# First loop of a four-layer graph network in fp32: the order of scores, attention times vectors, residual updates, low parts and stores

## The reference

```python
h = relu(layernorm(x))                                       # before each layer
x += softmax_over_nodes(rowsum((h Wq) * (adj (h Wk))) / sqrt(512)) * (h Wv)     # layer 0
w = adj * exp((h Wq + bq)(h Wk + bk)^T);  x += (w / rowsum(w)) (h Wv + bv)      # layer 1
x += Wo . attention with 8 heads, scores times 2 adj                            # layer 2
x += relu(H0 W0 + (T H) W1 + (T T H) W2 + biases), T from adj and a leaky relu  # layer 3
```

## Time and profile before

| | |
|---|---|
| median of 3 runs | 2211.23 us (2210.95 to 2213.39) |
| profiled execution | 2211.67 us, of it 2209.9 us from first to last instruction |
| TensorE busy | 2195.3 us, 99% |
| VectorE, ScalarE, GpSimd busy | 1306.4, 780.1, 721.7 us |
| granted TensorE clock | 1.00 |

### The profile page before, as it was taken

One profiled execution on the slowest core, in us unless ns is written; L12 is line 12 of the kernel. 1 busy time (PEld: TensorE's weight loads), 2 busy tenths in 40 slices (PEclk: granted clock), 3 DMA queues, 4 the chain that ended last, 5 costly groups with the idle time before them and its releaser, 6 DMA issues.

```text
span 2209.9 us, 39185 instructions
## 1 busy us (share of the span) xinstructions
PE 2195.3 (99%) x15756; PEld 1762.6 (80%) x15756; DVE 1306.4 (59%) x2712; ACT 780.1 (35%) x1393; POOL 721.7 (33%) x926
## 2 busy tenths in 40 slices
PE   8999999999999999999999999999999999999999
PEld 5788888888888888888888888888887777777776
DVE  4576666665665576655555555555676555555542
ACT  3433333233323333333332333332444444444432
POOL 1443433343443422432332323332353131213120
PEclk9999999999999999999999999999999999999999
DMA  6333323333333344433333323323452323232411
GB/s 211 78 80 98 101 84 98 90 93 92 86 93 94 106 136 127 113 86 93 86 101 95 112 82 91 92 82 101 139 162 81 120 73 121 74 120 72 123 46 58
DMA packets 142007, 220.53 MB, mean 100 GB/s; under 512 B 33920, under 2 KB 40064, under 8 KB 141824
## 3 DMA queue, kind: packets, MB, share of 16 engines
q1 hardware_dynamic: 135680, 209.62, 32.6%
q10 hardware_dynamic: 6144, 8.40, 1.6%
HBM read 84.71 MB, written 50.37 MB: 61 GB/s over the span
## 4 chain that ended last, share of the span: by engine, by line
PE 97%; SPq 1%; DMA 1%; DVE 1%; issue 0%; POOL 0%; ACT 0%; DVEq 0%; ACTq 0%
PE bank L327 54%; PE bank L317 32%; PE bank L343 3%; PE bank L563 2%; PE bank L499 1%; PE bank L469 1%; PE bank L364 1%; SPq L1001 1%; PE bank L307 1%; PE bank L549 0%; DVE hs L649 0%; DMA mcolt<-in_nodemask_cols 0%; DMA wq<-in_L_gnn_Wq_w 0%; DMA si<-rowsT 0%; DMA sirows<-si 0%
## 5 line engine op out<-in xcount | busy, mean ns | idle before, releaser
L327 PE MATMUL bank<-w_hi,h3T_hi 128*128 128x512 f32 x768 | 302.4, 394 | 0.0
L327 PE MATMUL bank<-w_hi,h3T_lo 128*128 128x512 f32 x768 | 299.0, 389 | 0.0
L327 PE MATMUL bank<-w_lo,h3T_hi 128*128 128x512 f32 x768 | 298.8, 389 | 0.0
L1008 ACT ACTIVATE Z<-bank 64x512 f32<-64x512 f32 x256 | 151.9, 593 | 273.3 <-PE bank L327 168.7
L624 DVE BATCH_NORM_STATS2 stA<-x 128x6 f32<-128x512 f32 x192 | 128.1, 667 | 114.8 <-DMA x<-in_x 106.5
L1022 ACT ACTIVATE hn<-x,stA 128x512 f32<-128x512 f32 x192 | 141.6, 823 | 119.1 <-POOL stA L1269 119.1
L649 DVE STREAM_TRANSPOSE hs<-hn 128x512 f32<-128x512 f32 x192 | 124.5, 690 | 87.6 <-ACT hn L1022 87.6
L327 PEld LDWEIGHTS bank<-w_hi,h3T_hi 128*128 128x128 f32 x768 | 144.1, 188 | 32.5 <-issue 1.6
L327 PEld LDWEIGHTS bank<-w_hi,h3T_lo 128*128 128x128 f32 x768 | 144.2, 188 | 30.4
L327 PEld LDWEIGHTS bank<-w_lo,h3T_hi 128*128 128x128 f32 x768 | 144.2, 188 | 29.9
L1077 ACT ACTIVATE QQ<-bank,bqk 128x512 f32<-128x512 f32 x64 | 43.9, 689 | 282.7 <-PE bank L317 246.9
(11 more groups left out here) (201 smaller groups left out, 5575.9 us busy)
## 6 DMA issues: line engine op xcount, KB each, us to landing
hGA<-hs SPq DMA_DIRECT2D x760, 64.0 KB, 2.0
mid<-x SPq DMA_DIRECT2D x32, 1024.0 KB, 4.3
x<-mid SPq DMA_DIRECT2D x32, 1024.0 KB, 5.7
x<-in_x SPq DMA_DIRECT2D x16, 1024.0 KB, 6.0
hGB<-hs SPq DMA_DIRECT2D x256, 64.0 KB, 2.0
out<-x SPq DMA_DIRECT2D x15, 1024.0 KB, 4.7
PT<-hs SPq DMA_DIRECT2D x120, 64.0 KB, 2.0
PT<-hs ACTq DMA_DIRECT2D x120, 64.0 KB, 2.1
```

What stands on the lines that cost most here:

```text
L327: ins = eng.matmul(b[:], h[l][:, k, ts], W[r][:, k, :], start=(k == 0 and i == 0), stop=(last and k == 3 and i == 2))
L1008: return eng.activation(dst, src, ACT.Copy)
```

## The change

TensorE, for g from 2 to 15: g0(g), g1(g-1), s0(g), pv(g-2), s1(g-1), v0(g, 0..3), v1(g-1, 0..3). Iteration 16: q2(0) whole, g1(15), pv(14), s1(15), v1(15, 0..3). Iterations 0 and 1 keep their order. VectorE: stats_A and the transposes of the next group come first (but at g = 1); x2(g-2) comes after p(g); the lo parts of h0T are made there from group 3 on, before the transposes of layer 1; the lo parts of Wq2 go from VectorE to GpSimd. ScalarE: hi parts of h1T between the g0 evictions, then norm_A, g1, the exponentials, norm_B(0), the hi parts of h0T, norm_B(1..3); the hi parts of Wk2 after the exponentials of group 15. SP: the gather of the next group ahead of the store of x(g-2).

```diff
@@ pe_program
             for g in range(NG + 1):
-                on0, on1, on_pv = g < NG, g >= 1, g >= 2
-                if on0:
+                if g < NG:
                     l01_g0(g, range(4))
...
-                if g == NG:
-                    l2_gemm_T("q2", 0, Wq2, a_q, (0,))
-                if on_pv:
+                else:
+                    l2_gemm_T("q2", 0, Wq2, a_q)
+                if g >= 2:
+                    l01_g1(g - 1)
+                    if g < NG:
+                        l01_s0(g)
                     l01_pv(g - 2)
...
+                    l01_s1(g - 1)
+                    if g < NG:
+                        for t in range(4):
+                            l01_v0(g, t)
+                    for t in range(4):
+                        l01_v1(g - 1, t)
+                    continue
...
@@ dve_program
+                if g < NG:
+                    k = (0, g + 1) if g + 1 < NG else (2, 0)
+                    stats_A(*k)
+                    if g != 1:
+                        transposes(*k)
+                else:
+                    stats_A(2, 1)
+                    transposes(2, 1)
                 if on0:
                     dve.wait_ge(*bank.done(("s0", g)))
...
                     l01_p(g)
-                    if g >= 2:
-                        transposes(*((0, g + 1) if g + 1 < NG else (2, 0)))
+                if on_pv:
+                    l01_x2(g - 2)
+                if on0:
                     xt = xs[x_slot(kA(0, g))]
...
+                    if g == NG - 1:
+                        features2_lo(0)
+                    elif g >= 2:
+                        features0_lo(g + 1, hT[0])
                     transposes(1, g)
                     if on1:
                         l01_dots(g)
-                    if g == NG - 1:
-                        split_in_place(Wq2, "q2")
-                        features2_lo(0)
@@ act_program
+                if g >= 2:
                     act.wait_ge(*bank.done(("v1", g - 2, 3)))
+                    features2_hi(1, g - 1, hT[1], (0, 1))
+                    if on0:
+                        g0(g, (0,))
+                        features2_hi(1, g - 1, hT[1], (2,))
+                        g0(g, (1,))
+                        features2_hi(1, g - 1, hT[1], (3,))
+                        g0(g, (2, 3))
+                        norm_A(*((0, g + 1) if g + 1 < NG else (2, 0)))
+                        g1(g - 1)
+                        if g == NG - 1:
+                            split_in_place(Wq2, d_q2)
+                        l01_zexp(g)
+                        l01_exp(g - 1)
+                        norm_B(g, (0,))
+                        act.wait_ge(*bank.done(("v0", g, 3)))
...
+                        norm_B(g, (1, 2, 3))
+                    else:
+                        features2_hi(1, g - 1, hT[1], (2, 3))
+                        l2_evict("q2", 0, QQ, 0, a_q)
+                        norm_A(2, 1)
+                        g1(g - 1)
+                        l01_exp(g - 1)
+                        split_in_place(Wk2, d_k2)
+                    continue
@@ pool_program
+                if g >= 2:
+                    l01_exadj(g - 1)
+                if g == NG - 1:
+                    split_in_place(Wq2, "q2")
...
-                    if g and g + 1 < NG:
-                        features_lo(0, g + 1, hT[0], hGA, p_flo0)
+                    if g == 1:
+                        features_lo(0, 2, hT[0], hGA, p_flo0)
@@ sp_program
-                if on_pv:
-                    sp.wait_ge(v_x2, 12 * (g - 2) + 12)
-                    store_x(kA(0, g - 2), mid[0][g - 2])
...
                 if on0:
                     gather(*((0, g + 1) if g + 1 < NG else (2, 0)))
+                if on_pv:
+                    sp.wait_ge(v_x2, 12 * (g - 2) + 12)
+                    store_x(kA(0, g - 2), mid[0][g - 2])
```

More of the change, by code:

```diff
@@ L293, in build @@
         hi_of = {n: 4 * i + 4 for i, n in enumerate(("m0", "v0", "a1", "v1", "q2", "k2", "v2", "o2", "w2", "w1", "w0"))}
-        lo_dve = {n: 4 * i + 4 for i, n in enumerate(("m0", "a1", "v1", "q2", "k2", "v2", "o2"))}
-        lo_pool = {n: 4 * i + 4 for i, n in enumerate(("v0", "w2", "w1", "w0"))}
+        lo_dve = {n: 4 * i + 4 for i, n in enumerate(("m0", "a1", "v1", "k2", "v2", "o2"))}
+        lo_pool = {n: 4 * i + 4 for i, n in enumerate(("v0", "q2", "w2", "w1", "w0"))}
         def pe_program(eng):
@@ L408, in l2_gemm_T, with l01_g1 @@
                 pe.wait_ge(v_flo2, 4 * g + 4)
-                pe.wait_ge(v_wlo, lo_dve[n])
+                if n == "q2":
+                    pe.wait_ge(p_wlo, lo_pool[n])
+                else:
+                    pe.wait_ge(v_wlo, lo_dve[n])
                 for m in ms:
                     gemm_T((n, g, m), W, hT2[g % 2], m, (freed, 4 * g + m + 1))
+            def l01_g1(g):
+                pe.wait_ge(p_flo1, 4 * g + 4)
+                pe.wait_ge(v_wlo, lo_dve["a1"])
+                for oc in range(4):
+                    gemm_T(("g1", g, oc), Wa1, hT[1], oc, (a_g1, 4 * g + oc + 1))
@@ L413, in pe_program, with l01_s0, l01_s1 @@
+            def l01_s0(g):
+                pe.wait_ge(a_g0, 4 * g + 4)
+                scores(("s0", g), gT[0], hGA, (v_am, g + 1))
+            def l01_s1(g):
+                pe.wait_ge(a_g1, 4 * g + 4)
+                scores(("s1", g), gT[1], hGB, (a_ex, 4 * g + 4))
             for g in range(NG + 1):
-                on0, on1, on_pv = g < NG, g >= 1, g >= 2
-                if on0:
+                if g < NG:
                     l01_g0(g, range(4))
-                    if not on_pv:
-                        l01_v0(g, 0)
@@ L419, in pe_program @@
-                if g == NG:
-                    l2_gemm_T("q2", 0, Wq2, a_q, (0,))
-                if on_pv:
-                    l01_pv(g - 2)
[L423 to L437, removed]
+                else:
+                    l2_gemm_T("q2", 0, Wq2, a_q)
@@ new lines, in pe_program @@
+                if g >= 2:
+                    l01_g1(g - 1)
+                    if g < NG:
+                        l01_s0(g)
+                    l01_pv(g - 2)
+                    l01_s1(g - 1)
[5 more added lines that the diff above has]
+                    continue
+                l01_v0(g, 0)
+                l01_s0(g)
+                for t in range(1, 4):
+                    l01_v0(g, t)
@@ L438, in pe_program @@
+                if g == 1:
+                    l01_g1(0)
+                    l01_v1(0, 0)
+                    l01_s1(0)
                     for t in range(1, 4):
-                        l01_v1(g - 1, t)
+                        l01_v1(0, t)
                 else:
@@ L650, in transposes, with features0_lo @@
                                   (hn1 if layer == 1 else hn)[t][:].rearrange("p (c b r) -> p c b r", c=4, b=4)).then_inc(v_tr, 1)
-            def features0_lo():
+            def features0_lo(g, h):
                 for q in range(4):
-                    dve.wait_ge(a_fhi[0], q + 1)
-                    lo_split(by_token(hT[0]["lo"], q), hGA[:, q], by_token(hT[0]["hi"], q)).then_inc(p_flo0, 1)
+                    dve.wait_ge(a_fhi[0], 4 * g + q + 1)
+                    lo_split(by_token(h["lo"], q), hGA[:, q], by_token(h["hi"], q)).then_inc(p_flo0, 1)
             def features2_lo(g):
@@ L722, in dve_program @@
             split_W(Wm0, "m0")
-            features0_lo()
+            features0_lo(0, hT[0])
             dve.wait_ge(*bank.done(("s0",)))
@@ L732, in dve_program @@
                 on0, on1, on_pv = g < NG, g >= 1, g >= 2
[L733 to L736, removed]
-                if g == NG - 1:
-                    stats_A(2, 0)
-                if on_pv:
-                    l01_x2(g - 2)
+                if g < NG:
[6 more added lines that the diff above has]
+                    transposes(2, 1)
                 if on0:
@@ L769, in dve_program @@
                         l01_dots(g)
-                    if g == NG - 1:
-                        split_in_place(Wq2, "q2")
-                        features2_lo(0)
-                else:
-                    stats_A(2, 1)
-                    transposes(2, 1)
+                else:
                     split_in_place(Wk2, "k2")
@@ L1085, in act_program, with l01_exp @@
             split_W(Wa1, "a1", (0, 1))
+            def l01_exp(g):
+                act.wait_ge(*bank.done(("s1", g)))
+                act.wait_ge(v_ec, g + 1)
+                bv = bank.of(("s1", g))
+                for r in range(4):
+                    eng.activation(ex[:, r, :], bv[:, r * 64:(r + 1) * 64], ACT.Exp,
+                                   bias=ecol[g % 2][:, 4 + r:5 + r]).then_inc(a_ex, 1)
             for g in range(NG + 1):
                 on0, on1 = g < NG, g >= 1
[L1089 to L1095, removed]
@@ L1096, in act_program @@
-                if on0 and g >= 2:
-                    act.wait_ge(*bank.done(("v1", g - 2, 3)))
-                    features2_hi(1, g - 1, hT[1])
+                if g >= 2:
```

(42 more changed lines are left out.)

## The result

| | before | changed |
|---|---|---|
| median | 2211.23 us | 2220.9 us (2220.48 to 2221.44, 5 runs) |
| ratio | | 1.0044, 95% interval 1.0033 to 1.0055 |
| profiled execution | 2211.67, span 2209.9 | 2221.44, span 2219.6 |
| granted TensorE clock, mean | 1.000 | 0.997 |

The changed kernel is 0.44% slower, 9.7 us; the forecast was 2221.4 (2214 to 2229).

What follows compares the result with a forecast made beforehand. TensorE, busy 99%, was taken as the bound. Joins -3.3, steady waits +0.5, iteration 2 +1.7, s1 +0.4, tail wait +8.9 and slow clock +2.0 gave +10.2 on 2211.2: 2221.4 us, range 2214 to 2229.

Steps and rivals of the forecast that it cites:

- What bounds: Whole kernel: TensorE, busy 99% of the span, gains only where its matmuls are more than 0.227 us apart.
- Joins: Small-matmul blocks s0, pv, s1 made one: 15 further joins at 0.22 us each, -3.3 us.
- The chain to h1T's low parts: Steady loop, s0 to g1: 24.1 us to the gather, about 0.4 us slack, waits of 0.5 us in all.
- Iteration 2: g1(1), now due right after g0(2), waits once for the late low part of h1T(1): +1.7 us.
- ScalarE ahead of s1: Iteration 16, without s0: s1 is due before ScalarE's g1 evictions end, +0.4 us (0 to 1.0).
- The tail: Iteration 16: Wv2's load goes out later, so pv(15) waits for vf(15, 3): +8.9 us (8.4 to 9.5).
- The clock: After the wait for vf(15, 3): slow matmuls at TensorE's lowered clock, +2.0 us (0 to 2.6).
- (a): Rival: Wv2's load stays hidden, so not slower; 2210.5 us, or 2209 without iteration 2's wait; chance 0.1.
- (b): Rival: the h1T chain takes 0.8 us longer and g1 waits in 14 iterations; +11 more, 2232 us; chance 0.13.
- (c): Rival: the joins are worth nothing, s0 to pv costing a full switch; 2224.7 us; chance 0.12.
- (d): Rival: faster outright, Wv2 hidden, joins worth double, no wait in iteration 2; 2205 us; chance 0.02.

Runs made afterwards that it cites:

- e5: e1 with TensorE running v0(g, 0) between pv(g-2) and s1(g-1) for g from 2 to 15, so s1 stands alone; 2212.73 us.
- e6: e1 with VectorE making the four low parts of h0T twice for groups 3 to 15; 2249.34 us in one execution.
- e7: e1 with the low parts of h0T for groups 3 to 15 kept on GpSimd, as in the kernel before; 2209.61 us.
- e4: e1 with the second half of gather (1,1) issued by ScalarE's queue beside SP's first half; 2208.49 us.
- e10: The changed kernel without any edit, measured again on the same chip as e9; 2221.22 us.
- e1: Changed kernel with Wv2's load issued ahead of the store of x(14) and gather (2,1) in iteration 16; 2209.84 us.
- e9: Changed kernel with 40 extra, overwritten TensorE matmuls ahead of its wait for vf(15,3); 2218.7 us.
- e8: e1 with SP's wait for x2(g-2) and store again ahead of the next group's gather, g from 2 to 15; 2311.68 us in one execution.
- e3: e1 with gather (2,1) also ahead of the wait for g1(15), so both gather and Wv2's load precede the store of x(14); 2213.74 us.

## Why the prediction was right

- **What bounds.** TensorE, which had no wait to give back. Right: every term that the profile after shows is a distance between its matmuls.
- **Joins**, -3.3 from 15 x 0.22: measured -3.5. e5 shows that the loop's gain is this and nothing else.
- **The chain to h1T's low parts**, 24.1 us to the gather: measured 24.03 to 24.05 in iterations 2 to 15. Slack +1.1 to -0.1 for fast and slow gathers: from the end of the last low part to g1 it was 1.2 us with a fast gather, less with slower ones, and 0.05, which is the signal alone, in the two iterations where g1 was late. Waits 0.5 in all: 0.6. e6 shows that VectorE's steps are in the chain. One term of the sum was too large: e7 takes the low parts of h0T out again, and the chain is 1.6 us shorter, not 2.4.
- **Iteration 2**, +1.7: measured +1.9, and 1.2 to 1.9 in the other profiles that have the wait. e4 takes most of it away.
- **ScalarE ahead of s1** in iteration 16, +0.4: measured nothing. g1's evictions ended at 836.29, s1 was due at 836.81; the gather was a fast one (10.02 us), the lower end of that term. In e10 a wait of 0.5 us stands there. The gather was as fast (10.01 us), but the load of x behind it took 6.6 us to land instead of 5.6, a spread that the term had put down to the gather alone.
- **The tail**, +8.9 in 8.4 to 9.5: measured 9.8, and 9.0 us of wait in e10. It is a little over the upper end. From pv(14) to pv(15) were 27.5 us, where the upper sum has 27.1: about 0.1 us more each between store and gather, between gather and Wv2's load, up to Wv2's hi parts (5.69 instead of 5.55) and for the signal to pv(15). In e10 the wait is shorter because s1 had taken 0.5 of it already. e1 shows the cause. The second half of the argument, that nothing in the second loop takes it back, held (10.2 us behind to its end); the third loop gave 0.5.
- **The clock**, +2.0 between 0 and 2.6: measured 1.5 in the profile, 2.5 between the profiles of e9 and e10. The granted clock of 1.00 in the first microseconds, which the prediction set against the weight loads, is not a measurement: in all twelve traces the records of the clock begin only at 10.6 to 13.8 us, and 0.4 to 0.8 us behind the first of them the weight loads are 0.43 us apart instead of 0.85. So the loads were the row to go by. The Trainium skill (TensorE: Matmul & The Clock Gate, "What's actually happening") has the clock fall when TensorE stands, and here the record shows it.
- **Rivals.** (a) would have needed Wv2 early: e1 builds it and measures 2209.84, against 2210.5 in the prediction. (b) needs 0.8 us more in the chain: the slack was there, and e6 and e8 are what it looks like without. (c) is excluded by the iterations of 49.65 us and by e5, (d) by the waits.

That the sum, +10.2 against +9.7, is better than its parts is luck: the tail was 0.9 too small, while the s1 term (0.4), the clock (0.5) and the third loop's 0.5 were on the other side.

## What to carry to other kernels

Where one engine is busy 99%, cost a reordering by what it makes due earlier, and follow each moved step into the queues that issue DMAs: the loss here came from one weight load that stood behind a store, which stood behind a result that had moved 19 us. Check the first and the last iterations by themselves; the steady loop had been arranged with a microsecond to spare, the seams had not. When an order is changed, let each load wait for the thing that it overwrites and for nothing else.

## What was not expected of the hardware

- A TensorE wait of 1.9 us (e3) halved the clock for some 3 us and slowed pv(15) as much as one of 9.7 us; waits of 0.9 to 1.7 us in iteration 2 were in no profile (one execution each) followed by slow matmuls, and of 13 waits of 1.7 to 2.5 us (e6) 5 were, among them one of 1.8 and not the longest. So in these profiles a short wait costs its length, one of about two microseconds up to nearly double.
- The half clock can come 0.9 to 1.5 us after TensorE has started again (in e6 matmuls 0.43 us apart from 338.35 on, after a wait that ended at 336.81).
- A gather of 16 DMAs takes 10.0 to 11.4 us to issue in the first loop of the kernel before, up to 12.2 in those of the others, and 11.1 to 12.5 right behind a store of 1 MB (e8).
